# Twenty of 36 probability tiles through memory in the first batch too, with the extra ring places laid over the FFN's tiles

## What is computed

```python
x = x + attn(layernorm(x));  x = x + ffn(layernorm(x))
# attn
q, k, v = (x @ Wq.T, x @ Wk.T, x @ Wv.T)        # heads of 128; q and k through an RMS norm
scores = einsum('bkgqd,bksd->bkgqs', q, k) / sqrt(128) + slope * (pos_k - pos_q)   # causal
out = softmax(scores) @ v;  return out @ Wo.T
# ffn
gate = 8 * softmax(x @ Wr.T + br);  low = einsum('bsd,hrd->bshr', x, A)
return 2 * einsum('bshr,hor,bsh->bso', low, B, gate)
```

## Time and profile before

| | us |
|---|---|
| median of three runs | 2074.18 (2071.1 to 2074.81) |
| profiled execution | 2071.61, of it span 2069.8 |
| TensorE busy | 2005.8 (97%) |
| DVE busy | 1374.0 (66%) |
| ACT busy | 1158.9 (56%) |
| POOL busy | 1158.9 (56%) |

### The profile page before, as it was taken

How to read it: one execution, slowest core, us unless ns; L and a number is a source line. 1 busy time by engine, 2 the same in 40 slices (tenths; PEclk the granted TensorE clock), 3 DMA queues, 4 the chain that set the end, 5 groups by cost and what they waited for, 6 DMA issues and landing times.

```text
span 2069.8 us, 33617 instructions
## 1 busy us (share of the span) xinstructions
PE 2005.8 (97%) x11068; PEld 1711.6 (83%) x11068; DVE 1374.0 (66%) x3431; ACT 1158.9 (56%) x3314; POOL 1158.9 (56%) x1160
## 2 busy tenths in 40 slices
PE   7999999999999999999999999999999999999996
PEld 6888888888888888888888888787888878788774
DVE  6656666566666666669876666565656656566686
ACT  4656656566555656556445565554555655565552
POOL 3554645646455564646635747465674746657473
PEclk9999999999999999999999999999999999999998
DMA  4463644546355363555445637365463746637254
GB/s 163 120 135 110 166 122 131 106 125 171 107 144 138 97 158 115 146 151 153 122 131 140 136 99 175 99 151 142 108 138 99 176 102 142 154 77 167 70 124 93
DMA packets 822668, 269.13 MB, mean 130 GB/s; under 512 B 618584, under 2 KB 766040, under 8 KB 822496
## 3 DMA queue, kind: packets, MB, share of 16 engines
q1 hardware_dynamic: 770592, 164.75, 37.8%
q10 hardware_dynamic: 51904, 102.24, 14.2%
HBM read 145.25 MB, written 121.63 MB: 129 GB/s over the span
## 4 chain that ended last, share of the span: by engine, by line
PE 79%; DVE 6%; issue 4%; SPq 3%; DMA 3%; POOL 3%; ACT 2%; DVEq 0%; POOLq 0%; ACTq 0%
PE s_ps L1077 17%; PE q_ps L1077 15%; PE o_ps L1077 14%; PE y_ps L1077 14%; PE turn_ps L1164 10%; PE turn_ps L1077 7%; SPq L626 3%; DMA p_bounce<-probs_odd 1%; POOL probs_odd L852 1%; DVE more_raw L958 1%; DVE p_raw L958 1%; DVE qn L983 1%; DMA more_raw<-p_bounce 1%; POOL more_lo L858 1%; ACT qn L782 1%
## 5 line engine op out<-in xcount | busy, mean ns | idle before, releaser
L852 POOL TENSOR_TENSOR probs_odd<-probs_odd,p_inv 128x256 f32<-128x256 f32 (+3 forms) x256 | 316.6, 1255 | 212.4 <-DVE p_inv L979 212.4
L852 POOL TENSOR_TENSOR probs_even<-probs_even,p_inv 128x128 f32<-128x128 f32 (+3 forms) x256 | 261.6, 1043 | 222.0 <-DVE p_inv L979 221.7
L858 POOL TENSOR_TENSOR pT_lo<-p_raw,pT_hi 128x512 fp32r<-128x512 f32 x176 | 232.5, 1328 | 150.2 <-ACT pT_hi L768 150.0
L972 DVE CUSTOM_DVE_ANT_0 probs_odd<-s_ps,rel 128x256 f32<-128x256 f32 (+3 forms) x256 | 209.4, 820 | 107.4 <-issue 106.1
L1077 PE MATMUL s_ps<-kT_hi,qT_hi 128*128 128x512 f32 (+3 forms) x768 | 276.9, 361 | 2.9 <-DVE neg_max L972 2.8
L1077 PE MATMUL s_ps<-kT_hi,qT_lo 128*128 128x512 f32 (+3 forms) x768 | 262.3, 342 | 0.0
L1077 PE MATMUL s_ps<-kT_lo,qT_hi 128*128 128x512 f32 (+3 forms) x768 | 261.7, 341 | 0.0
L773 ACT ACTIVATE probs_odd<-probs_odd,neg_max 128x256 f32<-128x256 f32 (+3 forms) x256 | 212.4, 831 | 64.7 <-DVE neg_max L972 63.4
L773 ACT ACTIVATE probs_even<-probs_even,neg_max 128x128 f32<-128x128 f32 (+3 forms) x256 | 184.5, 722 | 108.7 <-DVE neg_max L972 106.9
L972 DVE CUSTOM_DVE_ANT_0 probs_even<-s_ps,rel 128x128 f32<-128x128 f32 (+3 forms) x256 | 174.8, 687 | 102.6 <-issue 101.7
L950 DVE TENSOR_TENSOR pT_lo<-turn_ps,pT_hi 128x512 fp32r<-128x512 f32 x288 | 195.2, 680 | 52.7 <-ACT pT_hi L760 52.5
(11 more groups left out here) (123 smaller groups left out, 4880.1 us busy)
## 6 DMA issues: line engine op xcount, KB each, us to landing
p_raw<-p_bounce SPq DMA_DIRECT2D x896, 64.0 KB, 2.3
more_raw<-p_bounce SPq DMA_DIRECT2D x256, 64.0 KB, 2.2
p_bounce<-probs_even SPq DMA_DIRECT2D x64, 192.0 KB, 2.1
p_bounce<-probs_odd SPq DMA_DIRECT2D x32, 384.0 KB, 3.8
p_bounce<-probs_odd SPq DMA_DIRECT2D x32, 320.0 KB, 2.7
wq_kept<-wqT_hi ACTq DMA_DIRECT2D x8, 1024.0 KB, 4.4
wq_kept<-wqT_lo ACTq DMA_DIRECT2D x8, 1024.0 KB, 7.8
p_bounce<-probs_odd SPq DMA_DIRECT2D x64, 128.0 KB, 1.8
```

The source lines that it names most:

```text
L852: nc.gpsimd.tensor_tensor(row, row, p_inv[:, s % 2, h:h + 1].to_broadcast((P, L)), ALU.mult).then_inc(sems["normalise"], 1)
L858: nc.gpsimd.tensor_tensor(p_low(r), raw_p(raw_tile[w, s, j]), p_high(r).bitcast(F32), ALU.subtract).then_inc(sems["lower_p"], 1)
L972: nc.vector.tensor_tensor_reduce(out=probs[s % 2][:, h, 0:L], in0=s_ps[:, at_col:at_col + L], in1=rel[:, S - L:S], scale=-float(slopes[w % ...
```

## The change

Rounds 0 to 6 take 20 of 36 probability tiles through memory instead of 16: tile 2 of rows 4, 5 and 7 and tile 3 of row 6 change their way, so that rounds 0 to 6 have the same tiles as the second batch. Round 7 keeps its 16. There are now three stages (rounds 0 to 6, round 7, rounds 8 to 15). The always present places are 2 pairs and 3 raw tiles; stage 0 has one pair and two raw tiles more (`pT_hi_a`, `pT_lo_a`, `p_raw_a`), stage 2 two pairs and two raw tiles more (`..._b`). The places of stage 0 lie where `f_x`, `bT` and `arT` come from round 7 on, and the loads of A and Wr wait until their last users are done. All six tables are written anew. In all but `GROUP_A` they hold the same names as before in another order; in `GROUP_A` four `turn.p`, `high.p` and `low.p` give way to four `fetch_p`, `flip_p`, `upper_p` and `lower_p`.

```diff
-MEMORY_TILES = ({2: (2,), 3: (2, 3), 4: (3, 4), 5: (3, 4, 5), 6: (4, 5, 6), 7: (3, 4, 5, 6, 7)},
+MEMORY_TILES = ({2: (2,), 3: (2, 3), 4: (2, 3, 4), 5: (2, 3, 4, 5), 6: (3, 4, 5, 6), 7: (2, 3, 4, 5, 6, 7)},
+                {2: (2,), 3: (2, 3), 4: (3, 4), 5: (3, 4, 5), 6: (4, 5, 6), 7: (3, 4, 5, 6, 7)},
                 {2: (2,), 3: (2, 3), 4: (2, 3, 4), 5: (2, 3, 4, 5), 6: (3, 4, 5, 6), 7: (2, 3, 4, 5, 6, 7)})
...
 GROUP_A = (
...
-    "lower_p.7.4 low.p.7.2 flip_p.7.5 fetch_p.7.7 values.7.1 high.kv.3 values.7.2 inv_k values.7.3 flip_p.7.6 values.7.4 "
...
+    "lower_p.7.3 values.7.0 high.kv.3 flip_p.7.5 values.7.1 upper_p.7.4 flip_p.7.6 values.7.2 keep_wkv lower_p.7.4 "
+    "turn.q.8 load_wo values.7.3 inv_k high.q.8 q.9.1 upper_p.7.5 values.7.4 upper_p.7.6 flip_p.7.7 q.9.2 lower_p.7.5 "
...
-    MEMORY_SLOTS, RAW_TILES = (2, 4), (3, 5)
+    MEMORY_SLOTS, RAW_TILES = 2, 3
+    MORE_SLOTS, MORE_RAW = (1, 0, 2), (2, 0, 2)
...
+    def stage(w):
+        return 0 if w < NG - 1 else 1 if w < NG else 2
...
-        return list(MEMORY_TILES[w // NG].get(s, ()))
+        return list(MEMORY_TILES[stage(w)].get(s, ()))
...
+    def place(n, of, always, more):
+        n %= always + more[of]
+        return n if n < always else n + sum(more[:of])
...
-                p_slot[name] = TURN_SLOTS + flips[b] % MEMORY_SLOTS[b]
+                p_slot[name] = TURN_SLOTS + place(flips[of], of, MEMORY_SLOTS, MORE_SLOTS)
...
-                raw_tile[name] = fetches[b] % RAW_TILES[b]
+                raw_tile[name] = place(fetches[of], of, RAW_TILES, MORE_RAW)
...
-        arT = sb("arT", [P, C, P + NE])
-        bT = sb("bT", [P, DM])
-        f_x = sb("f_x", [P, 2, DM])
...
+        pairs_2 = [(sb(f"pT_hi_b{i}", [P, G * P], F32R), sb(f"pT_lo_b{i}", [P, G * P], F32R)) for i in range(MORE_SLOTS[2])]
+        raw_2 = [sb(f"p_raw_b{i}", [P, G * P]) for i in range(MORE_RAW[2])]
+
+        with nc.sbuf_tensor("f_x", [P, 2, DM], F32) as f_x, nc.sbuf_tensor("bT", [P, DM], F32) as bT, \
+                nc.sbuf_tensor("arT", [P, C, P + NE], F32) as arT:
+            pass
+        pairs_0 = [(sb(f"pT_hi_a{i}", [P, G * P], F32R), sb(f"pT_lo_a{i}", [P, G * P], F32R)) for i in range(MORE_SLOTS[0])]
+        raw_0 = [sb(f"p_raw_a{i}", [P, G * P]) for i in range(MORE_RAW[0])]
...
+        def ffn_place_free(engine):
+            for name in last_early_slots:
+                after(engine, "values", *name)
+            for name in last_early_raws:
+                after(engine, "lower_p", *name)
...
             def load_a(w):
+                ffn_place_free(sp)
                 sp.dma_start(f_x[:, 0, :], A.rearrange("h r d -> (h r) d")).then_inc(a_loaded, 16)
...
             def load_wr(w):
+                ffn_place_free(sp)
                 sp.dma_start(f_x[0:NE, 1, :], Wr).then_inc(wr_loaded, 16)
```

More of the change, by code:

```diff
@@ L21 @@
 BIG = 3e38
-MEMORY_TILES = ({2: (2,), 3: (2, 3), 4: (3, 4), 5: (3, 4, 5), 6: (4, 5, 6), 7: (3, 4, 5, 6, 7)},
+MEMORY_TILES = ({2: (2,), 3: (2, 3), 4: (2, 3, 4), 5: (2, 3, 4, 5), 6: (3, 4, 5, 6), 7: (2, 3, 4, 5, 6, 7)},
+                {2: (2,), 3: (2, 3), 4: (3, 4), 5: (3, 4, 5), 6: (4, 5, 6), 7: (3, 4, 5, 6, 7)},
                 {2: (2,), 3: (2, 3), 4: (2, 3, 4), 5: (2, 3, 4, 5), 6: (3, 4, 5, 6), 7: (2, 3, 4, 5, 6, 7)})
 PROLOGUE = (
[11 rows of a table removed]
[11 rows of a table added]
 )
 GROUP_A = (
[45 rows of a table removed]
-    "keep_wkv v_low add_y.7 "
[46 rows of a table added]
 )
 BOUNDARY = (
[60 rows of a table removed]
[60 rows of a table added]
 )
 FIRST_B = (
[47 rows of a table removed]
[47 rows of a table added]
 )
 GROUP_B = (
[43 rows of a table removed]
[43 rows of a table added]
     "add_y.7 "
@@ L386, in attention_lora_block @@
     turned, sends = [], [0, 0]
-    flips, fetches, last_in_slot, in_raw = [0, 0], [0, 0], {}, {}
+    flips, fetches, last_in_slot, in_raw = [0] * 3, [0] * 3, {}, {}
+    def place(n, of, always, more):
+        n %= always + more[of]
+        return n if n < always else n + sum(more[:of])
     for w in range(-1, LAST_W + 1):
@@ L393, in attention_lora_block @@
             elif item[0] == "flip_p":
-                name, b = (w, *item[1:]), w // NG
-                p_slot[name] = TURN_SLOTS + flips[b] % MEMORY_SLOTS[b]
+                name, of = (w, *item[1:]), stage(w)
+                p_slot[name] = TURN_SLOTS + place(flips[of], of, MEMORY_SLOTS, MORE_SLOTS)
                 p_before[name] = last_in_slot.get(p_slot[name])
                 last_in_slot[p_slot[name]] = name
-                flips[b] += 1
+                flips[of] += 1
             elif item[0] == "send_p" and item[2] == G - 1:
@@ L408, in attention_lora_block @@
                 raw_uses[name] = len(users)
-                fetches[b] += 1
+                fetches[of] += 1
     def follow(work):
@@ L450, in attention_lora_block @@
         qT_lo = sb("qT_lo", [P, 2, G, P], F32R)
-        p_raw = sb("p_raw", [P, RAW_TILES[0], G * P])
-        pT_hi = sb("pT_hi", [P, TURN_SLOTS + MEMORY_SLOTS[0], G * P], F32R)
-        pT_lo = sb("pT_lo", [P, TURN_SLOTS + MEMORY_SLOTS[0], G * P], F32R)
+        p_raw = sb("p_raw", [P, RAW_TILES, G * P])
+        pT_hi = sb("pT_hi", [P, TURN_SLOTS + MEMORY_SLOTS, G * P], F32R)
+        pT_lo = sb("pT_lo", [P, TURN_SLOTS + MEMORY_SLOTS, G * P], F32R)
         oT_hi = sb("oT_hi", [P, G, P], F32R)
         oT_lo = sb("oT_lo", [P, G, P], F32R)
-        arT = sb("arT", [P, C, P + NE])
-        bT = sb("bT", [P, DM])
-        f_x = sb("f_x", [P, 2, DM])
         f_logits = sb("f_logits", [P, 2, P + NE])
@@ L498, in attention_lora_block @@
             pass
-        more_hi = sb("more_hi", [P, 2, G * P], F32R)
-        more_lo = sb("more_lo", [P, 2, G * P], F32R)
-        more_raw = sb("more_raw", [P, 2, G * P])
+        pairs_2 = [(sb(f"pT_hi_b{i}", [P, G * P], F32R), sb(f"pT_lo_b{i}", [P, G * P], F32R)) for i in range(MORE_SLOTS[2])]
[5 more added lines that the diff above has]
+        raw_0 = [sb(f"p_raw_a{i}", [P, G * P]) for i in range(MORE_RAW[0])]
+        sb("arT_rest", [P, C * (P + NE) - W512])
+        turned_pairs = [(pT_hi[:, i, :], pT_lo[:, i, :]) for i in range(TURN_SLOTS + MEMORY_SLOTS)]
+        turned_pairs += [(hi[:], lo[:]) for hi, lo in pairs_0 + pairs_2]
+        raws = [p_raw[:, i, :] for i in range(RAW_TILES)] + [raw[:] for raw in raw_0 + raw_2]
         b_raw = f_x[:, 0, :].rearrange("p (h o r) -> p h o r", o=C, r=RK)
@@ L508, in p_high @@
         def p_high(slot):
-            more = slot - TURN_SLOTS - MEMORY_SLOTS[0]
-            return pT_hi[:, slot, :] if more < 0 else more_hi[:, more, :]
+            return turned_pairs[slot][0]
         def p_low(slot):
-            more = slot - TURN_SLOTS - MEMORY_SLOTS[0]
-            return pT_lo[:, slot, :] if more < 0 else more_lo[:, more, :]
+            return turned_pairs[slot][1]
         def raw_p(n):
-            return p_raw[:, n, :] if n < RAW_TILES[0] else more_raw[:, n - RAW_TILES[0], :]
+            return raws[n]
+        early = [name for name in p_slot if name[0] < NG - 1]
+        last_early_slots = [[name for name in early if p_slot[name] == TURN_SLOTS + MEMORY_SLOTS + i][-1] for i in range(MORE_SLOTS[0])]
+        last_early_raws = [[name for name in raw_tile if name[0] < NG - 1 and raw_tile[name] == RAW_TILES + i][-1] for i in range(MORE_RAW[0])]
+        def ffn_place_free(engine):
[3 more added lines that the diff above has]
+                after(engine, "lower_p", *name)
         def x_source(b, t):
@@ L550, in attention_lora_block @@
         p_sent = [sem("p_sent_even"), sem("p_sent_odd")]
-        p_fetched = [sem(f"p_fetched{i}") for i in range(RAW_TILES[1])]
+        p_fetched = [sem(f"p_fetched{i}") for i in range(RAW_TILES + sum(MORE_RAW))]
         ident_ready = sem("ident_ready")
```

## The result

The changed kernel takes 2100.09 us (median of four runs, 2098.9 to 2104.48) against 2072.64 (2069.42 to 2074.81) for the kernel before on the same chip: ratio 1.0138, 95% interval 1.0116 to 1.0159. It is slower by 1.4%, where 2060 was forecast. The profiled execution has a span of 2098.8 us, 29.0 more than before.

What follows compares the result with a forecast made beforehand. TensorE and its few waits were taken to bound the kernel. The terms -11.5 + 2 - 5 + 0 = -14.5 us gave 2057.1 on the profiled execution, 2059.7 on the median, say 2060 us; range 2050 to 2071.

Steps and rivals of the forecast that it cites:

- What bounds the kernel: Whole kernel: TensorE, busy 2005.8 of 2069.8 us, sets the time, with the few microseconds in which it stands still.
- Part 1: Rounds 0 to 6: 28 groups of four transposes leave TensorE at 0.41 us each, -11.5 us.
- Part 2: End of batch one's rounds: six fetched tiles, with spill and load beside the last, cost 0.3 us a round, +2 us.
- margin of "about 1 us": End of batch one's rounds: 31.0 us of TensorE's work against a 29.9 us chain to the last fetched tile.
- only the last of the six tiles meets the 2 MB: Row 7's fetches in batch one: wkv's spill and Wo's load go out beside the sixth tile alone.
- The third rival: Rounds 0 to 6: spill and Wo's load delay the last fetches 2.9 us a round, +8.8, 2083 us; chance 0.04.
- Part 3: Rounds 9 to 14: the same tiles in a new order cut waits by 0.8 us a round, -5 us.
- the chain of part 2: Round's end, from last score product through row 7's sends and fetches to the last value product: 29.9 us.
- One budget: Rounds 9 to 14: wait removed at row 7's first value product returns at its last; 2.2 us each.
- Part 4: Rounds 7, 8, 15 and the start: small gains and losses cancel, 0 us, ends -5 and +5.
- The rule against the change: Fetches' 128-byte runs: transfers under 512 B are penalised; with that price on top, 2104 us.
- the price in the row: Fetches: the measured row used these same 128-byte packets, so it already includes their cost and nothing is added.

Runs made afterwards that it cites:

- e1: Changed kernel with Wo's load moved back to mid-round and wkv's spill back to the round's end in rounds 0 to 6: 2063.17 us, ratio 0.9962.
- e9: e5 with DVE's turn of row 7's second fetched tile moved behind row 6's lower output half in rounds 9 to 14: 2059.80 us, ratio 0.9946.
- e5: e1 with the spill of Wo in round 7 moved earlier, away from the loads of x's tiles 4 and 6: 2056.92 us, ratio 0.9935.
- e3: Changed kernel with only wkv's spill moved back to the round's end, Wo's load staying among the last fetches: 2077.24 us, ratio 1.0037.
- e4: Kernel before, with 16 tiles in memory, but wkv's spill and Wo's load moved late among the last fetches: 2099.99 us, ratio 1.0141.

## Why the prediction was wrong

**What bounds the kernel**: right. TensorE and its few waits decide everything above.

**Part 1**: right, once the rest is taken away. The 24 groups in rounds 1 to 6 are worth 746.70 - 736.41 = 10.3 us in e1, 0.43 a group for the 0.41 taken. The forecast of 122.8 us busy in rounds of 123.6 to 124.2 holds for e1 (122.7 and 123.75), and up to the end of round 6 e1 is 11.9 us ahead of the kernel before, for -11.5. That the sum fits so well is in part luck: rounds 1 to 6 are 8.9 us shorter, since they idle 1.4 longer, and round 0 with the start is 3.0 shorter, more than its four groups.

**Part 2** is the step that failed, in "I charge 0.3 us a round". Rounds 0 to 6 are 24.6 us longer than before, where -9.5 was forecast. The margin of "about 1 us" was sound; the runs put it nearer 2. What it was held against was not. That "only the last of the six tiles meets the 2 MB" was nearly true (in two rounds the last transfer of the fifth is late too, at 3.7 and 3.8 us) and no comfort, since that tile ends the chain. Its lateness was read from one load of 1 MB with fetches issued beside it (2.9 us more); behind 2 MB it is 4.7 to 7.0. That gives 25.3 us of waits in seven rounds instead of 2, already beyond the far end of +18. And a term was missing from the sum: the low clock behind each wait, 2.2 us a round. In the trace of before no such wait stands in batch one, but round 10 could have shown it: it has a wait of 1.9 us and is busy for 119.95 us at a clock of 0.99, where its neighbours have 118.8 and 118.7.

**The third rival** named the mechanism, the place and the deciding point, got the price at half (2.9 us a round; waits and low clock came to 5.8), and had a chance of 0.04. What spoke for it in the trace (landings of 5 us beside one load, a margin of 1 us, twice the bytes) was worth more than that.

**Part 3**: -5 forecast, -0.6 measured. The failed step is "the chain of part 2 should be 1.7 us shorter". In round 9 of the changed kernel the last score product starts at 1307.01 and the last freed product at 1337.25, 30.2 apart, as before (1276.68 and 1306.95 in the earlier trace rows). The sends of row 7 still land late, since each pair goes out beside a fetch:

```profile
1309.60 1.02 SPq L641 DMA_DIRECT2D p_bounce<-probs_odd  x2
1310.72 3.31 SPq L652 DMA_DIRECT2D p_raw_b<-p_bounce  x4
1314.07 1.08 SPq L641 DMA_DIRECT2D p_bounce<-probs_odd  x2
1319.60 2.21 SPq L652 DMA_DIRECT2D p_raw_b<-p_bounce  x4
```

```profile
DMA to landing us min/median/max: 3.1/4.0/5.0
```

That is the second pair, against the earlier trace rows: the first fetch follows 4.45 us behind it, for 3.7 before. The 2.5 us were read from sends that left with nothing beside them. "One budget" was right (e9).

**Part 4**: 0 forecast, +5.5 in round 7. I followed the transposes and products of the new table and not its DMAs; the spill of Wo beside the loads of x is the fault of part 2 once more (e5).

**The rule against the change.** The measured 2100 lies near the 2104 that the rule would have given, but not by its mechanism. e1 moves the same 128-byte runs, with the DMA engines busier in rounds 1 to 6 than in either kernel of the change (0.61, for 0.51 before and 0.57 in the changed one), and takes 2063.17. The sum's choice to leave the price in the row was right.

## What to carry to other kernels

A transfer moved in one queue is a transfer moved past all others: before an order is changed, list what is in flight beside each large one, and ask which small transfer ends a chain there. A spill or a prefetch belongs behind the last critical landing of its stage, not beside it; that cost nothing here and was worth 37 us. Where TensorE is the bound, price a wait of 2 us or more at itself and add 1.3 to 2.4 us for the clock, which fell behind most such waits here.

## What the runs showed of the hardware

**Transfers of one queue hold up those of another.** A transfer of 64 KB in 128-byte runs, issued by SP, landed 9.4 us after its issue beside 2 MB from ACT's queue, and the 1 MB load beside it after 9.6, with the DMA engines at 1.01 of their time in the first 4 us. The Trainium skill (DMA: Bandwidth & Descriptors, Issuing engines are not separate DMA queues) says that transfers from all queues run on the same 16 engines and interleave. The trace agrees: the small one lands together with the large one, not ahead of it. That 1 MB of load delays a fetch by more than 1 MB of spill (5.9 to 7.2 us against 4.5 to 6.0) I had not expected.

**The clock falls after short waits.** In e3 the waits before the last value product were 1.89, 1.69 and 2.02 us in rounds 1, 4 and 6, with TensorE's busy time of these rounds at 122.9, and 1.85 in round 3 and 1.20 in round 5 with a second of 1.23 behind it, with 124.3 and 124.6. In e4 waits of 0.6 to 1.5 us left the round at 124.7 to 124.8, those of 2.6 to 4.5 made it 126.1 to 126.2. In the changed kernel a wait of 1.96 us (round 2) was followed by the low clock, and in batch two of e5 so were two waits of 1.07 and 0.92 us close together (two of 1.01 and 1.32 in round 13 of e1 were not):

```profile
1658.28 0.50 PE L1105 MATMUL o_ps<-pT_hi_b,v_hi 128*128 128x512 f32 x1 [1.07 <-POOL pT_lo_b L886]
...
1660.16 0.75 PE L1105 MATMUL o_ps<-pT_hi_b,v_hi 128*128 128x512 f32 x1 [0.92 <-POOL pT_lo_b L886]
1660.71 0.63 PE L1105 MATMUL o_ps<-pT_lo_b,v_hi 128*128 128x512 f32 x1
```

So a wait of about 2 us may or may not bring the clock to 0.50, whatever caused it (a DMA in batch one, DVE in round 7), and it costs 1.3 to 2.4 us on top. The Trainium skill (TensorE: Matmul & The Clock Gate, What's actually happening) says that the gate knows two levels, half and full; the stretches above agree (0.50 and 1.00, with values between only where a stretch holds both).
